# A two-layer decoder on one core: one wait per round of four keys, SiLU on ScalarE, batch loops written out

## What is computed

```python
x = _layernorm(x + _L0_attn_ref(x, ...))      # 16 heads, neighbours up to 3 away
x = _layernorm(x + _L0_xattn_ref(x, mask, ctx_1024, ...))
x = _layernorm(x + _L0_ffn_ref(x, ...))       # 8 experts, top 2
x = _layernorm(x + _L1_attn_ref(x, ...))      # keeps the 32 best keys
x = _layernorm(x + _L1_xattn_ref(ctx_1024, ctx_1024, x, ...))
x = _layernorm(x + _L1_ffn_ref(x, ...))       # shared expert + 8 experts, GELU
```

```python
# _L0_xattn_ref, the gate: 77 context keys for every token
h = jnp.tanh(txt_proj[:, None, :, :] + feat_proj[:, :, None, :] + b[None, None, :, :][..., 0, :])
rho = jnp.einsum('bftd,d->bft', h, w[:, 0])
# _L0_ffn_ref: every expert on every token, weighted by the router
g, u = jnp.split(x @ gup.T, 2, axis=-1)
acc = acc + ce[:, None] * (jax.nn.silu(g) * u @ dn.T)
```

## Time and profile before

| | us |
|---|---|
| median of 3 runs (lowest, highest) | 893.12 (892.77, 893.54) |
| the profiled execution | 892.3 |
| its span in the profile | 889.9 |
| mean granted TensorE clock | 0.922 |

### The profile page before, as it was taken

How to read it: one execution, slowest core, us unless ns; L and a number is a source line. 1 busy time by engine, 2 the same in 40 slices (tenths; PEclk the granted TensorE clock), 3 DMA queues, 4 the chain that set the end, 5 groups by cost and what they waited for, 6 DMA issues and landing times.

```text
span 889.9 us, 12254 instructions
## 1 busy us (share of the span) xinstructions
PE 747.6 (84%) x4056; PEld 516.2 (58%) x4056; DVE 587.2 (66%) x1548; ACT 385.8 (43%) x634; POOL 76.5 (9%) x71
## 2 busy tenths in 40 slices
PE   3468678989988988999988979899988999973596
PEld 1221156876245966776246857775347878852586
DVE  3568467885765677775755787864946687749344
ACT  1058632237875432237875432257864322211142
POOL 2100020110011120100011120100011000000100
PEclk8769979999998999999999999999998999987578
DMA  6025000000000010000000010000000000000000
GB/s 239 0 71 201 1 27 1 1 1 1 1 3 1 1 42 1 1 1 1 1 3 1 2 41 1 1 1 1 1 3 1 1 13 1 1 1 0 1 1 12
DMA packets 6558, 15.13 MB, mean 17 GB/s; under 512 B 2776, under 2 KB 2912, under 8 KB 6240
## 3 DMA queue, kind: packets, MB, share of 16 engines
q1 hardware_dynamic: 6496, 14.32, 4.8%
HBM read 13.27 MB, written 1.05 MB: 16 GB/s over the span
## 4 chain that ended last, share of the span: by engine, by line
issue 66%; PE 14%; DVE 10%; POOL 7%; ACT 1%; DMA 1%; SPq 1%; POOLq 0%; DVEq 0%; ACTq 0%
PE bank L643 3%; PE bank L602 2%; PE bank L504 1%; POOL b_rstd L1407 1%; PE bank L505 1%; PE bank L506 1%; POOL a_big L1417 1%; DVE a_big L1382 1%; DVE top L1265 1%; POOL b_y L1433 1%; DVE b_big L1269 1%; DVE gup_lo L1362 1%; POOL a_sum L1420 1%; POOL a_rstd L1403 1%; DMA rb_sb<-rb 1%
## 5 line engine op out<-in xcount | busy, mean ns | idle before, releaser
L878 ACT ACTIVATE b_big<-bank 128x512 f32<-128x512 f32 x128 | 75.7, 596 | 207.2 <-PE bank L506 207.1
L847 ACT ACTIVATE a_big<-a_sum,txt_cols 128x512 f32<-128x512 f32 x231 | 145.5, 712 | 14.2 <-PE bank L602 14.1
L602 PE MATMUL bank<-a_big,score_pad 128*32 128x512 f32 x616 | 143.9, 616 | 7.4 <-ACT a_big L967 5.8
L1227 DVE SCALAR_TENSOR_TENSOR b_big<-b_big,bank 128x512 f32<-128x512 f32 x128 | 87.3, 682 | 63.9 <-ACT b_big L878 59.9
L643 PEld LDWEIGHTS bank<-down_sb,b_big 128*128 128x128 f32 x1024 | 118.2, 192 | 6.1 <-issue 3.5
L504 PE MATMUL bank<-x_hi,gup_hi 128*128 128x512 f32 x256 | 112.4, 439 | 9.5 <-DVE b_big L1227 5.9
L643 PE MATMUL bank<-down_sb,b_big 128*128 128x128 f32 x1024 | 119.9, 276 | 0.0
L505 PE MATMUL bank<-x_hi,gup_lo 128*128 128x512 f32 x256 | 103.6, 405 | 0.0
L506 PE MATMUL bank<-x_lo,gup_hi 128*128 128x512 f32 x256 | 103.5, 404 | 0.0
L1233 DVE TENSOR_TENSOR b_big<-bank,b_big 128x512 f32<-128x512 f32 x128 | 88.5, 692 | 4.4
L602 PEld LDWEIGHTS bank<-a_big,score_pad 128*32 128x32 f32 x616 | 28.3, 109 | 101.2 <-ACT a_big L847 54.7
(11 more groups left out here) (215 smaller groups left out, 960.7 us busy)
## 6 DMA issues: line engine op xcount, KB each, us to landing
b_big<-gup SPq DMA_DIRECT2D x8, 512.0 KB, 6.5
down_sb<-down SPq DMA_DIRECT2D x1, 2048.0 KB, 8.2
rw_sb<-rw SPq DMA_DIRECT2D x1, 1152.0 KB, 10.4
a_T<-x_T SPq DMA_DIRECT2D x4, 256.0 KB, 2.6
a_tok<-x_tok SPq DMA_DIRECT2D x4, 256.0 KB, 3.1
b_big<-rw SPq DMA_DIRECT2D x2, 512.0 KB, 3.6
y<-b_tok SPq DMA_DIRECT2D x4, 256.0 KB, 2.0
const_sb<-const SPq DMA_DIRECT2D x1, 872.0 KB
```

The lines of the kernel that those rows point to most:

```text
L602: last = mm(P[2][32 * j:32 * j + 32, :], score_pad[:, 31 - i:63 - i], ring[k % RING], start=(i == 0), stop=(KCOL * (i + 1) + j >= KEYS))
L847: act(ring[k % RING], a_sum[:, 0:S], ACT.Tanh, bias=txt_cols[:, c:c + 1])\
L878: act(th[n % 3], P[3 + 2 * (c % 2)][:, :], ACT.Tanh, scale=0.5).then_inc(th_ready, 1)
L1227: stt(th[n % 3], th[n % 3], 1.0, P[3 + 2 * (c % 2)][:, :], ALU.add, ALU.mult)\
```

## The change

Three edits. (1) PE waits for the tanh of a whole round before its first key and for none between its keys. (2) ACT applies SiLU to the gate half itself (`ACT.Silu`), so DVE's L1227 and its semaphore `t1_done` are gone; a gate bank is now freed by ACT's `th_ready`; the router weights lose their factor 0.5. (3) The loops over batches are Python loops, so all waits are on constants, and there are no branches.

```diff
--- before.py
+++ after.py
@@ -379,7 +379,6 @@
         g_psum = sem("g_psum")
         u_psum = sem("u_psum")
         th_ready = sem("th_ready")
-        t1_done = sem("t1_done")
         hid_ready = sem("hid_ready")
         down_psum = sem("down_psum")
         part_ready = sem("part_ready")
@@ -483,7 +482,7 @@
             eng.wait_ge(x_lo_ready, 1)
             eng.wait_ge(logit_psum, 1)
             load_a(1)
-            with eng.Fori(0, B - 2) as b:
+            for b in range(B - 2):
                 load_context(b + 1)
                 eng.wait_ge(x_lo_ready, b + 2)
                 eng.wait_ge(logit_psum, 2 * b + 3)
@@ -594,11 +593,11 @@
             def gate_scores(b, first, end):
 
                 for i in range(first, end):
+                    eng.wait_ge(tanh_ready, KEYS * b + min(KCOL * i + KCOL, KEYS))
                     for j in range(KCOL):
                         k = KCOL * i + j
                         if k >= KEYS:
                             continue
-                        eng.wait_ge(tanh_ready, KEYS * b + k + 1)
                         last = mm(P[2][32 * j:32 * j + 32, :], score_pad[:, 31 - i:63 - i], ring[k % RING],
                                   start=(i == 0), stop=(KCOL * (i + 1) + j >= KEYS))
                     last.then_inc(rho_round, 1)
@@ -647,7 +646,7 @@
                 for e in range(E):
                     for c in range(C0):
                         n = e * C0 + c
-                        for half, bank, freed, ready in ((0, P[3 + 2 * (c % 2)], t1_done, g_psum),
+                        for half, bank, freed, ready in ((0, P[3 + 2 * (c % 2)], th_ready, g_psum),
                                                          (1, P[4 + 2 * (c % 2)], hid_ready, u_psum)):
                             if n >= 2:
                                 eng.wait_ge(freed, E * C0 * b + n - 1)
@@ -797,7 +796,7 @@
             gate_to_tokens(0)
             turn_x2(0)
             logits_x2(0)
-            with eng.Fori(0, B - 1) as b:
+            for b in range(B - 1):
                 second_half(b, True)
             second_half(B - 1, False)
 
@@ -875,7 +874,7 @@
                         eng.wait_ge(g_psum, E * C0 * b + n + 1)
                         if n >= 3:
                             eng.wait_ge(hid_ready, E * C0 * b + n - 2)
-                        act(th[n % 3], P[3 + 2 * (c % 2)][:, :], ACT.Tanh, scale=0.5).then_inc(th_ready, 1)
+                        act(th[n % 3], P[3 + 2 * (c % 2)][:, :], ACT.Silu).then_inc(th_ready, 1)
                         if n == 0:
                             route_exp(b, 0)
                         if ahead:
@@ -1202,8 +1201,7 @@
                 eng.reciprocal(r_den[:, :], r_den[:, :]).then_inc(share_step, 1)
                 eng.wait_ge(share_step, n + 3)
 
-                stt(r0_we, r0_we, 0.5, r_den[:, :].unsqueeze(2).broadcast_to(r_wide), ALU.mult, ALU.mult)\
-                    .then_inc(r_weights, 1)
+                tt(r0_we, r0_we, r_den[:, :].unsqueeze(2).broadcast_to(r_wide), ALU.mult).then_inc(r_weights, 1)
 
 
             def swiglu(b, ahead):
@@ -1224,9 +1222,6 @@
                     for c in range(C0):
                         n = e * C0 + c
                         eng.wait_ge(th_ready, E * C0 * b + n + 1)
-                        stt(th[n % 3], th[n % 3], 1.0, P[3 + 2 * (c % 2)][:, :], ALU.add, ALU.mult)\
-                            .then_inc(t1_done, 1)
-                        eng.wait_ge(t1_done, E * C0 * b + n + 1)
                         eng.wait_ge(u_psum, E * C0 * b + n + 1)
                         if c == 0 and e >= 2:
                             eng.wait_ge(down_psum, E * b + e - 1)
```

## The result

The changed kernel takes 886.93 us (885.00 to 887.53, 4 runs) beside 893.33 us for the kernel before in the same session: ratio 0.9921, interval 0.990 to 0.9942. Forecast was 885.8 in a range of 875 to 895. The profiled execution of the changed kernel took 887.53 us, its span is 885.7. The profiled execution of before took 892.3, with a span of 889.9.

The account below looks back on a forecast made before the run. No engine is full; PE's waits, mostly ended by DVE in swiglu, and ACT's tanh pace in the gate stages set the limit. Terms -6.3 - 5.1 - 1.5 - 3.2 + 1.8 - 0.6 + 1 + 3.6 + 3 = -7.3 gave 885.0, median 885.8, range 875 to 895.

Parts of the forecast that it names:

- The waits at n = 6: Swiglu, batches 0 to 2: removing DVE's instructions shortens PE's waits before the head scores, 6.3 of 7.4 us gained.
- The clock behind them: Swiglu, after n = 6: the 1.2 GHz stretch disappears in three batches, 3 x 1.7 = 5.1 us gained.
- Batch 3: Gate half of n = 2: 0.7 us moves forward, half a chance the following low clock disappears; 1.5 us gained.
- Loads at n = 10: Swiglu: exp's table loads make n = 13 wait 1.15 us, but waits at n = 15 and 24 go; 3.2 us gained.
- Exp of the cross attention: A 1.28 us table load before this exp covers a 0.68 us wait and adds 0.6; +1.8 over three batches.
- (d): Rival: a switch of tables costs the drain of the skill's page, making the kernel slower, about 898 us; chance 0.05.
- The loops: Batch starts: PE's branch is off the path behind the mask's DMA; only SP's register instructions go, 0.6 us gained.
- the +1: Batch starts: PE stands idle 2.5 to 3 us at a stretch, so a low clock may follow, costing 1 us.
- up to 1.9 each: Lower end of the loops step: gain to be had at batch starts should the mask's DMA come earlier.
- 0 at full clock: Gate rounds: with one wait per round, a round ends when it ended before, so nothing behind it moves.
- The clock of the rounds: Bursts lower PE's clock: +3.6 us in top and cross attention (1.2 per batch), +3 in the prologue.
- Rival (b): The clock falls in every gate stretch, price 20.6 us: slower, 898 us, 899 on the median; chance 0.12.

Follow-up runs that it names:

- a wait per key: Changed kernel with PE again waiting for each key's tanh before its matmul, SiLU and written-out loops kept: 873.84 us, ratio 0.9773 to the kernel before.
- runs with fillers: Changed kernel plus one unused matmul before the wait of each prologue round and of rounds 8 to 12 in top attention: 879.63 us, ratio 0.9844.
- two keys in a piece: SiLU and written-out loops as in the changed kernel, but one wait for every two keys instead of four: 873.64 us, ratio 0.9778.

## Why the prediction was right, and where its steps were not

**The waits at n = 6** (-6.3 of 7.4). The mechanism was right. The number was a slip that came out well: by the working 0.6 us stays in each batch, which leaves 5.6, yet the sum took 6.3. What stays is 0.38, 0.38 and 0.36, so 6.3 were gained.

**The clock behind them** (-5.1). Right: the window from n = 6 on is at 1.00 in all three batches, where it was 0.50, and PE runs 20 records in the 3.40 us that held 12.

**Batch 3** (-1.5). Near in size (-1.67), by another split: PE's wait at n = 2 fell from 2.98 to 2.09 us, all of the 0.7 and a little more, and the low clock behind it stayed (0.71 for 5.9 us), on which I had put half. The other versions with SiLU show 82.22 to 83.91 us for this stage, so one execution's -1.67 says little.

**Loads at n = 10** (-3.2 net). This term failed, and it is the 2 us that swiglu gave less. The gate half of n = 8 stood 26.20, 26.36 and 25.73 us behind the start of swiglu in batches 0 to 2 before, and 23.55, 22.32 and 22.18 after; from there to the end of the stage the changed kernel gains only 0.4 us a batch, 1.2 in all. The gate half of n = 8 in batch 1, before and after:

```profile
342.93 0.51 PE L504 MATMUL bank<-x_hi,gup_hi 128*128 128x512 f32 x1
```

```profile
338.87 0.50 PE L503 MATMUL bank<-x_hi,gup_hi 128*128 128x512 f32 x1
```

Of the waits, 1.15 was foretold at the gate half of n = 13 and 1.03 came, with refill 1.19. But a wait of 0.16 follows at a down product, and the output projection, which was to come earlier, still waits 1.44 us for DVE in place of 1.78. The brackets of this part add up to 2.63 us, where 2.55 stood before. (The working has a small slip too: from 182.03 to 181.45 is 0.58, not 0.64.) It also took the loads for a price that has to be paid. Moving them by one step is worth 5 us in swiglu: the earlier trace rows shows 4.37 us of idle ACT directly ahead of them.

**Exp of the cross attention** (+0.6 each). Right: 19.13 us with loops alone, 19.76 with SiLU and loops.

**A drain behind the loads** (d). The Trainium skill, "ScalarE: Activation LUTs", section "What ACT_TABLE_LOAD costs", counts 2.66 us for a switch with its drain. Here the load of 155.22 takes 1.28 us and exp starts at 156.51, 0.01 us behind it; the trace disagrees.

**The loops** (-0.6, and the +1). This step failed. The forecast took the mask's DMA as a cover that comes when it comes, "whatever PE does". SP issued it at the same time indeed (3.35 us after the start of the last down product, before and with PE's loop written out), and it still ended the projection's wait: in the changed kernel it was issued at 317.68 and took 3.1 us, the projection starts at 320.85. But it landed sooner. The DMA queues of a 20 us window around the start of batch 1, the mask's transfer with its time to landing in the last column, before and with PE's loop alone written out:

```profile
q8 instruction: 2, 0.03, 0.7%
...
mask_sb<-key_mask SPq DMA_DIRECT2D x1, 40.0 KB, 4.1
```

```profile
q8 instruction: 1, 0.02, 0.3%
...
mask_sb<-key_mask SPq DMA_DIRECT2D x1, 40.0 KB, 3.0
```

4.1 and 4.8 us for batches 1 and 2 became 3.0 and 2.7. With SiLU it is the same: 4.6 and 3.8 in loops, 3.1 and 3.2 written out. With PE's branch there is one transfer of instructions more on the same DMA engines in that window. That this transfer delays the mask is argued from these rows, not shown by a run of its own. The second half of the miss is DVE's branch of 1.94 us, which was counted at n = 6; but with loops alone written out the waits there do not shrink. The lower end of the step, "up to 1.9 each", was nearer: 1.5 and 1.2 us of the -3.0 in the gelu row of the stages' table stand at the two ends of gelu where PE's branch was. The +1 for a low clock at batch starts was met by another way: batches 1 and 2 show nothing of it, but batch 0 starts swiglu behind the slower prologue at 0.56, with a wait per key at 0.70, and stands 0.9 us later at n = 2.

**The round wait, "0 at full clock".** Right. One round does wait visibly now, the last one in swiglu of batches 0 to 2, as here in batch 0 of the changed kernel, where the keys before went in one by one behind ACT.

```profile
225.20 1.06 PE L601 MATMUL bank<-a_big,score_pad 128*32 128x512 f32 x8 [1.82 <-ACT a_big L846]
```

It costs nothing: in the changed kernel and with a wait per key the swiglu stages of batches 1 and 2 are equal within 0.3 us, and the 0.9 of batch 0 are already there at n = 2.

**The clock of the rounds** (+3.6 and +3). The mechanism was right, the term for top and cross attention was too small: +9.4 measured, of which 1.7 are exp's load, so 7.7 for 3.6, at a clock of 0.90, 0.81 and 0.85 in place of 0.99. I had argued that the tanh on ACT and the search on DVE cover most of it. They do not: half of the 7.7 is in cross attention (22.81 us in batch 1 at 0.70, with a wait per key 19.75), the other half in top attention itself (34.20 us in batch 2 at 0.82, with a wait per key 31.07). The losses differ much from batch to batch under the same code. The prologue's +3.4 met the +3. By the experiment that undoes it, the whole of the round wait costs 13.1 us on the medians (13.6 by spans: 4.1 prologue, and in batches 0 to 2 7.7 top and cross, 0.7 swiglu and 1.2 gelu; batch 3 in all -0.1), and 6.6 had been given for it.

So the number came out right by luck: a missed gain (the loops, 8 us by the medians, 4 by the spans) stood against a loss that was 6.5 us too small (the round wait) and a SiLU gain that was 2 too large. Rival (b), the clock falling in every gate stretch, was more than half true: 11.8 us in the stages that it names, of its full 20.6. The Trainium skill, "TensorE: Matmul & The Clock Gate", in the section on PSUM-queue depth-cycling, tells of a kernel whose small idles between groups of matmuls make the clock fall and rise again; the runs with fillers and with two keys in a piece agree with it.

## What to carry over

Fewer waits were no gain here on an engine that follows a slower one. Small matmuls that went out as their operands came kept TensorE's clock at 0.93 and above; the same work gathered in bursts lost 13 us, and one useless matmul before 34 of the bursts brought 7 of them back. Writing out TensorE's loop alone gave nothing, TensorE's and VectorE's together gave 5 to 8 us: one engine's loop alone is no sufficient test. After a change of activation function look where its table loads fall, and move them into a wait of ScalarE that the profile already shows.

## What was not expected of the hardware

- Score matmuls in four column groups overlap when all four are ready (8 records in 1.06 us); with a wait for each two keys the 8 records of a round take 2.00 us in the prologue, with a wait for each key 2.27. The same 616 records are 103.7 us busy in the one form and 143.9 in the other. Busy time of PE is thus no measure of its work here.
- A table load starts while the operand of its activation is still being made (146.33 against 147.72 us). The load can lie in a wait for data. Where the activation has two waits, as SiLU at n = 11, the load carries the first (`hid_ready`) and the activation the second.
- A transfer of 40 KB landed 1.1 to 2.1 us sooner when TensorE's loop was written out, with one instruction transfer fewer around it; that the one causes the other was not tested.
- The clock depends on how the same work is spread: 154 records in 46.8 us at 0.93, or in 51.3 at 0.74.
